# Post-norm decoder layer on one core: FFN sums placed ahead of the convolution wait, Winograd terms made by batch, and first loads of the output stage issued in the last attention group

## Chip, cores, metric

One Trainium2 chip, one core. The metric is the device time of one execution in microseconds, the median of the runs shown. All data are fp32 in DRAM; products on TensorE run in fp32 or, where a value is split in a high and a low part, as three products of parts (type fp32r).

## What is computed

The reference, cut to what matters. x is (4, 1024, 512), ctx (4, 2048, 512).

```python
def attn(x):                       # 32 heads of 16 columns, over 1024 tokens
    q = lin(lin(x, wq), vq); k = lin(lin(x, wk), vk); v = lin(lin(x, wv), vv)
    o = softmax(q k^T / 4) v       # laid out again so that heads become rows
    return lin(o, wo_w, wo_b)
def xattn(z1ss, uss, z0, weight, bias):
    z1h, z1c = z1ss[:, :512], z1ss[:, 512:]
    conv = causal conv of z1h along the last axis, 2 taps, 512 -> 2048 channels
    it, ot, gt, ft = split(uss + conv + bias, 4)
    ct = sigmoid(ft) * shifted(z1c) + sigmoid(it) * tanh(gt)
    return concat([sigmoid(ot) * tanh(ct), ct], axis=1)
def ffn(x):
    x_int = clip(round(x / scale), -127, 127)
    return (x_int * scale) @ (ternary_weight - 1).T + bias
x = layernorm(x + attn(x))
x = layernorm(x + xattn(x, ctx, z0, weight, bias))
x = layernorm(x + ffn(x))
```

## The kernel before, in words

`combine` and `project` make q, k and v. `attend` then runs 64 slots (a head of a pair of batches each) in 16 groups of four, the first and the last group written out and the middle ones in a loop. In each slot TensorE makes scores, DVE the negative maxima (L510), ACT the exponentials (L490), TensorE the products with v (L425), and ACT copies the result out (L479). Every pair of slots is also normalised beside this: `store_out` (L620) writes a result to DRAM, `load_pair` (L630, L634) reads its sums and its values back, DVE takes reciprocals (`recips`, L667), `load_recips` (L642, L645) sends them through DRAM to spread them over the partitions, and POOL multiplies and splits (`normalise`, L673 to L679). `store_parts` (L660) writes the parts. The last pair, number 31, is left to `finish`: its `load_pair` and `load_recips` are issued there by SP, its `recips` is DVE's first and its `normalise` one of POOL's first instructions.

The order in SP's queue is written out by hand. At the end of `attend`, behind the four slots of the last group, SP waits for v_ready and issues wo_raw (L386), then four loads of attention parts of 1 MB each (`load_o`, L687), the last `store_parts` of the even pairs and the last `store_out`. In `finish` it issues x tiles 0 to 3 (L830), wo_bias and z0s (L892, L893), x tiles 4 to 7, `load_pair`, three constants (L899), `load_recips`, the ternary weight (L901, into the buffer of the gates), attention parts for tiles 8 to 11, x tiles 8 to 15, the last `store_parts`, parts for tiles 12 to 15, two convolution weights (L843) and then the ctx tiles (L839).

`finish` has two passes p of two batches. A pass is a stage of 16 output tiles (`wo_stage`) and 16 convolution steps (`convs`).

In `wo_stage` TensorE makes a tile of 128 tokens x 512 columns with 12 products (L149) into one of six banks. POOL adds the bias to x (`add_wob`, L961), two tiles ahead of the tile that it normalises. DVE adds this to the bank (L1224), takes statistics (L1205, L1206); POOL makes the inverse deviation in four small instructions (`inv_std`, L952 to L957); ACT applies it (L1041). A ring of four y buffers ties them: DVE may start tile n once tile n - 4 is applied. In pass 1 the last FFN tiles of pass 0 stand between the output tiles, at places given by the tables `FFN_AFTER` (DVE, ACT, POOL) and `FFN_SLOT` (TensorE); x tiles of pass 1 are read into places that an FFN tile sets free, and their bias is added at the places of `X_AT`.

The convolution is done in Winograd form over pairs of columns. For each of four channel blocks c it needs x1's even and odd columns and two differences. POOL makes one difference (`last_term`, L989), DVE the other (`first_term`, L1256), ACT the high parts (`high_parts`, L1076, L1079), DVE the low parts (`low_parts`, L1262, L1266). One block covers both batches (128x512) and starts with tile 14; blocks 2 and 3 come behind tile 15. TensorE's first convolution waits for the blocks one by one (wx_made).

In `convs` step s makes gate g = s % 4 of channel block m = s // 4 (36 products, L149). DVE adds both Winograd halves to the ctx tile (L1302, L1305), ACT applies sigmoid or tanh (L1098); at g = 2 the cell is made (L1309 to L1311) and at g = 3 the hidden value (L1316), each followed by two normalisations (L1323 and on). FFN tiles q run along with an offset: DVE rounds x (`rounded`, L1215, L1216) at s - 3, ACT makes integers (L1048), TensorE turns them (L1127) at step s - 5, ACT copies them (`copy_turned`, L1054), TensorE multiplies with the ternary weight (L1137) at s - 6 of a later step, DVE adds (`out_of_ffn`, L1234), POOL adds the FFN bias to x (`add_ffb`, L967). TensorE waits before an FFN product for the copy and for DVE's sum of the tile before (there is one bank).

DVE, ACT and POOL each issue in program order, so an instruction that waits holds back all behind it.

## Time and profile before

| | us |
|---|---|
| median of 3 runs | 2242.64 |
| the runs | 2240.01, 2242.64, 2259.2 |
| the profiled execution | 2237.79 |
| its span, first to last instruction | 2236.1 |
| TensorE matmul busy | 2105.0 (94%) |
| VectorE busy | 1657.5 (74%) |
| ScalarE busy | 1312.2 (59%) |
| GpSimd busy | 483.6 (22%) |
| mean granted TensorE clock | 0.966 |

Times inside the kernel are counted from the span's start. Attention ends at 1735; the two output stages begin at 1736 and 1969. PE is TensorE's matmul, PEld its weight loads, DVE VectorE, ACT ScalarE, POOL GpSimd, SP the engine that issues the DMAs. A busy share of TensorE counts instructions in flight, also at a lowered clock.

### The profile page before, as it was taken

What the parts mean: (1) busy time and instruction counts of PE and PEld (TensorE: products, weight loads), DVE (VectorE), ACT (ScalarE), POOL (GpSimd) and SP (SyncE); (2) the same over time, 40 slices, a digit from 0 to 9 for tenths busy, and PEclk for the clock granted to TensorE, in tenths of its full rate; (3) what the DMA queues carried; (4) which work ended last, traced back from release to release, by engine and by line L of the source; (5) the groups of instructions that cost most, each with busy time, mean ns of one, the idle gap of its engine ahead of it and who ended that gap; (6) DMA issues with size and microseconds to landing.
All of it is one profiled execution on the core that took longest, in us unless ns stands there. A gap on an engine that the chain in (4) does not pass through costs nothing.

```text
span 2236.1 us, 39953 instructions
## 1 busy us (share of the span) xinstructions
PE 2105.0 (94%) x11304; PEld 1188.6 (53%) x11304; DVE 1657.5 (74%) x1693; ACT 1312.2 (59%) x2405; POOL 483.6 (22%) x964
## 2 busy tenths in 40 slices
PE   8999996999999999999999999999999888988895
PEld 3788883444444444444444444444443666766663
DVE  3333326888899899999999999999994466675676
ACT  0121110777888888888888888888888133343343
POOL 0000000112212212212212222222221523463243
PEclk9999995999999999999999999999999999999997
DMA  4355547364665665664665665565553957653662
GB/s 155 95 169 150 150 150 96 59 131 112 117 132 114 117 133 114 116 134 112 117 135 112 116 135 112 116 136 112 115 126 109 336 190 258 239 194 120 214 221 71
DMA packets 205962, 315.20 MB, mean 141 GB/s; under 512 B 105168, under 2 KB 105168, under 8 KB 193616
## 3 DMA queue, kind: packets, MB, share of 16 engines
q1 hardware_dynamic: 205904, 314.47, 55.0%
q8 instruction: 31, 0.51, 0.1%
q14 instruction: 27, 0.22, 0.0%
HBM read 211.06 MB, written 101.19 MB: 140 GB/s over the span
## 4 chain that ended last, share of the span: by engine, by line
PE 65%; DVE 7%; POOL 5%; SPq 2%; DMA 2%; issue 2%; ACT 2%; DVEq 0%; POOLq 0%; ACTq 0%
PE psum L416 25%; PE psum L425 22%; PE psum L398 10%; PE psum L149 7%; POOL rstd L955 1%; DVE neg_max L510 1%; POOL x L961 1%; DVE stats L1205 1%; ACT gates L1098 1%; SPq L317 1%; POOL var_eps L952 1%; POOL neg_mean_rstd L957 1%; DMA attended_dram<-out 1%; PE psum L1137 1%; SPq L323 1%
## 5 line engine op out<-in xcount | busy, mean ns | idle before, releaser
L510 DVE TENSOR_REDUCE neg_max<-psum 128x1 f32<-128x1024 f32 x1024 | 1205.0, 1219 | 141.5 <-PE psum L398 141.3
L490 ACT ACTIVATE probs<-psum 128x512 f32<-128x512 f32 x2048 | 1066.0, 605 | 312.7 <-PE psum L416 312.5
L416 PE MATMUL psum<-q_op,k_op 50*128 50x512 f32 x2048 | 757.6, 450 | 8.0 <-ACT probs L490 5.2
L416 PEld LDWEIGHTS psum<-q_op,k_op 50*128 50x128 f32 x2048 | 355.2, 192 | 585.9 <-ACT probs L490 575.6
L398 PE MATMUL psum<-k_op,q_op 48*128 48x512 f32 x2048 | 630.6, 488 | 21.8 <-DMA k_op<-qk_parts_dram 14.3
L425 PE MATMUL psum<-probs,v_op 128*32 128x512 f32 x4096 | 547.2, 606 | 1.6
L398 PEld LDWEIGHTS psum<-k_op,q_op 48*128 48x128 f32 x2048 | 388.7, 315 | 51.0 <-DVE neg_max L510 19.1
L149 PE MATMUL psum<-x_wino,conv_w 128*128 128x512 f32 x1152 | 278.4, 401 | 17.9 <-DVE x_wino L1266 17.3
L149 PEld LDWEIGHTS psum<-x_wino,conv_w 128*128 128x128 f32 x1152 | 220.9, 194 | 66.9 <-issue 16.9
L557 POOL CAST neg_max_parts<-neg_max 128x8 fp32r<-128x8 f32 x128 | 24.2, 189 | 807.2 <-DVE neg_max L510 807.2
L425 PEld LDWEIGHTS psum<-probs,v_op 128*32 128x32 f32 x4096 | 82.5, 108 | 130.5 <-issue 67.6
L230 ACT ACTIVATE qk_parts<-psum,qk_bias 128x512 fp32r<-128x512 f32 x64 | 44.0, 688 | 166.1 <-PE psum L149 166.0
L243 DVE SCALAR_TENSOR_TENSOR qk_parts<-psum,qk_bias,qk_parts 128x512 fp32r<-128x512 f32 x64 | 48.0, 750 | 120.1 <-ACT qk_parts L230 120.1
L1041 ACT ACTIVATE x<-y,neg_mean_rstd,rstd 128x512 f32<-128x512 f32 x64 | 52.2, 816 | 141.8 <-POOL neg_mean_rstd L957 141.8
L547 POOL COPY v_op<-values 128x256 f32 (+1 forms) x64 | 25.4, 397 | 456.0 <-issue 344.1
L149 PE MATMUL psum<-x_hi,w_hi 128*128 128x512 f32 x256 | 102.0, 398 | 5.0 <-ACTq L224 5.0
L1302 DVE TENSOR_TENSOR gates<-psum,gates 128x1024 f32<-128x1024 f32 x32 | 38.9, 1216 | 89.0 <-PE psum L149 89.0
L149 PE MATMUL psum<-x_lo,w_hi 128*128 128x512 f32 x256 | 101.7, 397 | 0.0
L149 PE MATMUL psum<-x_hi,w_lo 128*128 128x512 f32 x256 | 101.6, 397 | 0.0
L952 POOL TENSOR_TENSOR var_eps<-mean_var,eps 128x1 f32<-128x1 f32 x96 | 26.5, 276 | 248.0 <-DVE mean_var L1206 247.9
L673 POOL TENSOR_TENSOR o_raw<-o_raw,recips 128x512 f32<-128x512 f32 x32 | 41.0, 1280 | 166.0 <-DMA recips<-recips_dram 166.0
L1137 PE MATMUL psum<-tern,x_int_t 128*128 128x512 bf16 x128 | 39.3, 436 | 36.9 <-DVE y L1234 29.4
(96 smaller groups left out, 1656.6 us busy)
## 6 DMA issues: line engine op xcount, KB each, us to landing
q_op<-qk_parts_dram SPq DMA_DIRECT2D x384, 128.0 KB, 4.0
conv_w<-conv_w_parts_dram SPq DMA_DIRECT2D x32, 1536.0 KB, 7.1
qk_parts_dram<-qk_parts SPq DMA_DIRECT2D x128, 256.0 KB, 3.1
k_op<-qk_parts_dram SPq DMA_DIRECT2D x384, 64.0 KB, 3.9
conv_w_parts_dram<-conv_w_parts SPq DMA_DIRECT2D x16, 1536.0 KB, 6.1
attended_dram<-out SPq DMA_DIRECT2D x64, 256.0 KB, 2.1
attended_parts_dram<-o_parts SPq DMA_DIRECT2D x128, 128.0 KB, 2.2
gates<-in_ctx_dram SPq DMA_DIRECT2D x32, 512.0 KB, 3.6
```

The lines of the kernel that those rows point to most:

```text
L149: mm = nc.tensor.matmul(out, left, right, start=(first and i == 0), stop=(last and i == n - 1))
L230: nc.scalar.activation(parts[j % 4][:, 0, :], bank[j % 6], ACT.Identity, bias=qk_bias[:, j // KC, j % KC:j % KC + 1]).then_inc(qk_hi, 1)
L243: nc.vector.scalar_tensor_tensor(out=parts[j % 4][:, 1, :], in0=bank[j % 6], scalar=qk_bias[:, j // KC, j % KC:j % KC + 1], in1=parts[j % ...
L398: return nc.tensor.matmul(s1_bank[t % 2][:, lane * HALF:(lane + 1) * HALF], qop[i][r, b, t:S:QT], kop[i][r, b, :], start=True, stop=True)
L416: nc.tensor.matmul(s2_bank[cell % RING], kop[i][r, j // 2, n // 2 * P:(n // 2 + 1) * P], qop[i][r, j // 2, j % 2 * HALF:(j % 2 + 1) * HALF ...
L425: mm = nc.tensor.matmul(pv_bank[32 * j:32 * j + 32, :], vop[k % 2][:, j // 2 * QT + kt, :], probs[n % DEEP][:, j, :], start=(n == 0), stop ...
L490: nc.scalar.activation(probs[n % DEEP][:, j, :], s2_bank[cell % RING], ACT.Exp, scale=SCALE).then_inc(exp_done, 1)
L510: nc.vector.tensor_reduce(mx[b][:, t:t + 1], s1_bank[t % 2][:], AX_X, ALU.max, negate=True).then_inc(maxed, 1)
L673: nc.gpsimd.tensor_tensor(norm["o"][:], norm["o"][:], norm["den"][:], ALU.mult).then_inc(norm["o_made"], 1)
L952: G.tensor_tensor(veps[:, r:r + 1], mv[:, r, 1:2], eps[:], ALU.add).then_inc(prep, 1)
L1041: A.activation(dst, y[r][:], ACT.Identity, bias=nmr[:, r:r + 1], scale=rstd[:, r:r + 1]).then_inc(normed, 1)
L1137: mm = nc.tensor.matmul(bank[7], xit[q % 2][:, kc, :], wt[:, kc, :], start=(kc == 0), stop=(kc == KC - 1))
```

## The change

Three things are done. (1) In slot 62 (`last and k == 2`) SP issues wo_raw and the four loads of attention parts, which stood behind slot 63, and then wo_bias and the four x tiles of the first four output tiles, into a buffer of their own (x_first, which lies where the gates' buffer has its second half); the ternary weight is loaded behind slot 63, once wo_lo is made, and turned to bf16 by DVE at the end of `attend`. POOL adds the bias to the first four x tiles before it waits for anything else, and then stays three tiles ahead. (2) The Winograd terms are made for one batch at a time, in pieces of 128x256: batch 0's from tile 9 on, between the output tiles. (3) The FFN instructions of a convolution step stand at its start instead of at its end, DVE's sum ahead of its rounding and POOL's inverse deviation ahead of its bias addition, with the offsets raised by one; ACT's copy of the turned integers keeps its place beside the other two and so comes one convolution step later. The tables of the second output stage follow.

The core of the diff:

```diff
@@ attend, SP, in slot()
+                    if last and k == 2:
+                        sp.wait_ge(v_ready, SLOTS)
+                        sp.dma_start(late["wo_raw"][:], wo_t.rearrange("(c p) n -> p c n", p=P)).then_inc(late["wo_in"], DMA)
+                        sp.wait_ge(norm["parts_stored"], PAIRS // 2 * PART_STORES + DMA)
+                        for n in range(2):
+                            load_o(sp, late, on_scr, 0, n)
+                        sp.dma_start(late["wo_bias"][:], wo_b.broadcast_to([P, F])).then_inc(late["wo_bias_in"], DMA)
+                        for t in range(KC):
+                            sp.dma_start(late["x_first"][:, t, :], x_nat[0, (KC + t) * P:(KC + t + 1) * P, :])\
+                                .then_inc(late["x_in"], DMA)
@@ attend, SP, behind the slots
-                sp.wait_ge(v_ready, SLOTS)
-                sp.dma_start(late["wo_raw"][:], wo_t.rearrange("(c p) n -> p c n", p=P)).then_inc(late["wo_in"], DMA)
-                sp.wait_ge(norm["parts_stored"], PAIRS // 2 * PART_STORES + DMA)
-                for n in range(2):
-                    load_o(sp, late, on_scr, 0, n)
+                sp.wait_ge(late["wo_made"], 1)
+                sp.dma_start(late["tern_raw"][:], tern_t.rearrange("(c p) n -> p c n", p=P)).then_inc(late["tern_in"], DMA)
@@ attend, DVE, behind wo_lo
+                dve.wait_ge(late["tern_in"], DMA)
+                nc.vector.tensor_scalar(late["tern"][:], late["tern_raw"][:], -1.0, None, ALU.add)\
+                    .then_inc(late["tern_made"], 1)
@@ finish, tables
-    FFN_AFTER = ({}, {1: 16, 3: 17, 5: 18, 7: 19, 8: 20})
-    FFN_SLOT = ({}, {0: 16, 2: 17, 5: 18, 7: 19, 9: 20, 10: 21})
+    FFN_AT = ({}, {0: 16, 3: 17, 4: 18, 6: 19, 8: 20, 11: 21})
+    FFN_SLOT = ({}, {0: 16, 3: 17, 5: 18, 7: 19, 9: 20, 11: 21})
@@ finish, SP
-                for pos in range(4):
-                    load_x(0, *wo_tile(pos))
-                sp.dma_start(wob[:], wo_b.broadcast_to([P, F])).then_inc(wob_in, DMA)
-                sp.dma_start(z0s[:], z0).then_inc(wob_in, DMA)
                 for pos in range(4, 8):
                     load_x(0, *wo_tile(pos))
+                sp.dma_start(z0s[:], z0).then_inc(z0_in, DMA)
                 load_pair(sp, norm, us_scr, PAIRS - 1)
...
-                sp.dma_start(wi, tern_t.rearrange("(c p) n -> p c n", p=P)).then_inc(tern_in, DMA)
@@ finish, POOL
                 def ffn_part(p, s):
+                    if s >= 6:
+                        inv_std("ffn", p, s - 6)
                     if 0 <= s - 4 < TILES:
                         add_ffb(p, s - 4)
-                    if s >= 5:
-                        inv_std("ffn", p, s - 5)
...
                     for i, pos in enumerate(ORDER[p]):
-                        if p == 0 and i + 2 < TILES:
-                            add_wob(0, *wo_tile(i + 2))
+                        if p == 0 and 4 <= i + 3 < TILES:
+                            add_wob(0, *wo_tile(i + 3))
                         if p == 1 and i in X_AT:
                             add_wob(1, *ffn_tile(X_AT[i]))
+                        if i in FFN_AT[p]:
+                            ffn_part(p - 1, FFN_AT[p][i])
                         inv_std("wo", p, pos)
-                        if i in FFN_AFTER[p]:
-                            ffn_part(p - 1, FFN_AFTER[p][i])
-                        if i >= 14:
-                            last_term(p, i - 14)
-                    last_term(p, 2)
-                    last_term(p, 3)
+                        if i >= 9:
+                            last_term(p, (i - 9) // KC, (i - 9) % KC)
+                    last_term(p, 1, 3)
@@ finish, ACT
-                def ffn_first(p, s):
+                def ffn_part(p, s):
+                    if 0 <= s - 5 < TILES:
+                        copy_turned(p, s - 5)
                     if 0 <= s - 4 < TILES:
-                        copy_turned(p, s - 4)
-
-                def ffn_rest(p, s):
-                    if 0 <= s - 3 < TILES:
-                        integers(p, s - 3)
-                    if s >= 5:
-                        q = s - 5
+                        integers(p, s - 4)
+                    if s >= 6:
+                        q = s - 6
...
                 def convs(p):
                     for s in range(CONVS):
                         m, g = s // 4, s % 4
-                        ffn_first(p, s)
+                        ffn_part(p, s)
                         act.wait_ge(gate_in, p * CONVS + s + 1)
...
-                        ffn_rest(p, s)
@@ finish, TensorE, first convolution of a pass
-                                pe.wait_ge(wx_made, p * KC + c + 1)
+                                pe.wait_ge(wx_made, (2 * p + 1) * KC + c + 1)
@@ finish, DVE
                 def ffn_part(p, s):
-                    if 0 <= s - 3 < TILES:
-                        rounded(p, s - 3)
-                    if s >= 5:
-                        out_of_ffn(p, s - 5)
+                    if s >= 6:
+                        out_of_ffn(p, s - 6)
+                    if 0 <= s - 4 < TILES:
+                        rounded(p, s - 4)
...
                 def wo_stage(p):
                     for i, pos in enumerate(ORDER[p]):
+                        if i in FFN_AT[p]:
+                            ffn_part(p - 1, FFN_AT[p][i])
                         out_of_wo(p, pos)
                         if p == 0 and i == 5:
                             constants()
-                        if i in FFN_AFTER[p]:
-                            ffn_part(p - 1, FFN_AFTER[p][i])
-                        if i >= 14:
-                            first_term(p, i - 14)
-                    low_parts(p, 0)
-                    first_term(p, 2)
-                    low_parts(p, 1)
-                    first_term(p, 3)
-                    low_parts(p, 2)
-                    low_parts(p, 3)
+                        if i >= 10:
+                            low_parts(p, (i - 10) // KC, (i - 10) % KC)
+                        if i >= 9:
+                            first_term(p, (i - 9) // KC, (i - 9) % KC)
+                    low_parts(p, 1, 2)
+                    first_term(p, 1, 3)
+                    low_parts(p, 1, 3)
...
                 def convs(p):
                     for s in range(CONVS):
                         m, g = s // 4, s % 4
+                        ffn_part(p, s)
...
-                        ffn_part(p, s)
```

`first_term`, `low_parts`, `last_term` and `high_parts` take the batch bi as an argument and work on `x1[:, bi, c, ...]`, `tmp(bi, c, v)` and `wx[v][part][:, c, bi, :]`, each 128x256; wx_made counts 16 in place of 8. ACT's `high_parts` stand from tile 9 on too, behind the tile's own normalisation.

## Rows read from the trace of the kernel before

**Rows 1.** Busy time of each engine by stretch; columns: us, busy (instructions), PEclk, DMA share, GB/s.

```profile
1735.00:1790.00 55.00, 46.41 (x191) 37.86 (x192) 24.11 (x50) 10.18 (x13) 34.38 (x75) 0.91 0.89 327
...
1790.00:1811.00 21.00, 10.76 (x40) 8.07 (x39) 15.61 (x22) 9.86 (x16) 11.52 (x19) 0.84 0.12 38
```

**Rows 2.** The chain that ended last, 1735 to 1757; start us, us, what.

```profile
1735.40 8.12 DMA attended_dram<-out
...
1743.59 6.41 DMA sums<-attended_dram
...
1750.46 2.18 DMA recips_dram<-sums
...
1752.72 3.73 DMA recips<-recips_dram
...
1756.53 1.30 POOL o_raw L673
```

**Rows 3.** A quiet DMA queue before 1734: landing, two lines of the timeline, one stretch.

```profile
attended_dram<-out SPq DMA_DIRECT2D x1, 256.0 KB, 2.0
...
1700.03 0.67 SPq L630 DMA_DIRECT2D sums<-attended_dram  x1
...
1702.75 0.34 DVE L667 RECIPROCAL sums<-sums 128x32 f32<-128x32 f32 x1
...
1710.00:1714.00 4.00, 3.10 (x20) 1.06 (x16) 0.00 (x0) 2.93 (x7) 0.00 (x0) 1.00 0.00 0
```

**Rows 4.** POOL's timeline; then groups of 1735 to 1812 and one tile's (min/median/max ns).

```profile
1759.92 1.09 POOL L961 TENSOR_TENSOR x<-x,wo_bias 128x512 f32<-128x512 f32 x1
...
1788.58 1.09 POOL L961 TENSOR_TENSOR x<-x,wo_bias 128x512 f32<-128x512 f32 x1
...
L961 POOL TENSOR_TENSOR x<-x,wo_bias 128x512 f32<-128x512 f32 x16 | 18.9, 1187 | 10.6 <-DMA z0s<-in_z_dram 10.6
...
L1205 DVE BATCH_NORM_STATS2 stats<-y 128x6 f32<-128x512 f32 x16 | 11.1, 694 | 0.5
...
L1266 DVE TENSOR_TENSOR x_wino<-gates,x_wino 128x512 fp32r<-128x512 f32 x8 | 6.0, 784 | 0.0
...
L1291 DVE TENSOR_TENSOR scale<-scale 128x1 f32<-128x1 f32 x1 | 0.2, 158 | 0.0
...
L1266 DVE TENSOR_TENSOR x_wino<-gates,x_wino x8: 676/678/1525, 1797.4 to 1807.6; 128x512 fp32r<-128x512 f32 x8
```

**Rows 5.** DVE: the last tile of the first stage; all of L1302, first and last start.

```profile
1792.55 0.68 DVE L1224 TENSOR_TENSOR y<-psum,x 128x512 f32<-128x512 f32 x1
...
L1302 DVE TENSOR_TENSOR gates<-psum,gates x32: 1204/1223/1226, 1811.0 to 2203.8; 128x1024 f32<-128x1024 f32 x32
```

**Rows 6.** POOL and DVE at 2034.5, timeline.

```profile
2034.53 2.49 POOL L989 TENSOR_TENSOR gates<-x 128x512 f32<-128x512 f32 x2
...
2034.59 1.53 DVE L1256 TENSOR_TENSOR gates<-x 128x512 f32<-128x512 f32 x1
```

**Rows 7.** One group of four convolution steps, timeline.

```profile
1869.36 1.23 DVE L1302 TENSOR_TENSOR gates<-psum,gates 128x1024 f32<-128x1024 f32 x1 [4.42 <-PE psum L149]
...
1870.46 0.58 ACT L1054 COPY x_int_t<-psum 128x512 bf16<-128x512 bf16 x1 [3.37 <-PE psum L1127]
...
1881.53 1.86 PE L1137 MATMUL psum<-tern,x_int_t 128*128 128x512 bf16 x4 [2.84 <-DVE y L1234]
...
1881.70 0.81 ACT L1041 ACTIVATE x<-y,neg_mean_rstd,rstd 128x512 f32<-128x512 f32 x1 [0.54 <-POOL neg_mean_rstd L957]
...
1883.58 8.85 PE L149 MATMUL psum<-x_wino,conv_w 128*128 128x512 f32 x36
```

**Rows 8.** Second output stage, timelines of TensorE and DVE.

```profile
1977.82 1.02 PE L1137 MATMUL psum<-tern,x_int_t 128*128 128x512 bf16 x4 [2.74 <-DVE y L1234]
...
2015.60 0.69 DVE L1224 TENSOR_TENSOR y<-psum,x 128x512 f32<-128x512 f32 x1 [2.68 <-POOL x L961]
...
2046.72 1.22 DVE L1302 TENSOR_TENSOR gates<-psum,gates 128x1024 f32<-128x1024 f32 x1 [2.67 <-PE psum L149]
```

131 lines of the change are left out of this document (69 added, 62 removed).

## The prediction

> **What bounds the kernel now.** I read the busy time by stage first [rows 1]. Attention ends at 1735; behind it TensorE is still the fullest engine, so time can come only from stretches in which it sits idle or runs at the lower clock. The largest are the first output stage (46.4 of 55 us busy, granted clock 0.91) and the hand-over to the convolutions at 1790 to 1811 (10.8 of 21 us), which comes again in the second half. Within the convolutions TensorE loses a few us in each group of four steps.
>
> The chain of waits says why the first output stage is late [rows 2]: the last head's result takes 8.12 us to reach DRAM, its sums 6.41 us to come back, the reciprocals 2.18 and 3.73 us. POOL can scale that last head pair only at 1756.53, and every normalisation of the output stage is queued behind this multiplication on POOL. On a quiet queue the same transfers are short: the same store landed in 2.0 us, and sums issued at 1700.03 were there for the reciprocal at 1702.75; from 1710 to 1714 the DMA engines moved nothing [rows 3]. That is the hole the change fills. From 1760 POOL sets the pace: from the bias addition at 1759.92 to that at 1788.58 lie twelve tiles, so 2.4 us a tile, of which the addition is 1.19 and the inverse deviation 1.2 [rows 4].
>
> **Part 1, loads moved into the last attention group.** Moved to SP behind the last stored maxima (about 1706): the output weight, four loads of attention parts, the bias, four x tiles: 1 + 4 + 0.25 + 1 MB. The busy stretch moved 327 GB/s at a share of 0.89 [rows 1], so 0.37 MB a us at full share: 17 us, until about 1723. Then follow conv_w (1.5 MB), the ternary weight (1 MB) and the parts: drained near 1732. SP passes ten issues of about 1 us each, in a stretch in which it only waited for the result at 1717; the reciprocals of pair 30 come a few us later, with more than 5 us of slack. The added wait (wo_made) has the ternary load, one store_parts and the last store_out behind it; DVE, idle there, has made the weight parts by about 1713, so I take 0, with 1 us as the upper bound and 0 below, since nothing is taken off attention itself.
>
> What it buys: the last store finds a quiet queue and lands near 1737.5, before SP asks for it. SP issues four x loads and z0 first, until about 1739. Sums then take 2.7 to 3.5 us, so the reciprocal is at about 1742.2; 2.2 + 3.7 us for the recips put POOL's multiplication at 1748.3, 8.2 us sooner. Two additions that no longer stand behind it give 2 x 1.19 = 2.4. TensorE's stall before tile 8 goes too, but POOL is the bound there. POOL scales tile 8 at 1748.3 + 3.4 (the pair, 1756.53 to 1759.92) + 1.2 + 8 x 2.35 = 1771.7, and with ACT's 0.8 it is ready at 1772.5.
>
> **Part 2, Winograd terms by batch, inside the stage.** 16 DVE pieces of 128x512 a pass become 32 of 128x256, ACT 12 become 24, POOL 4 become 8. No such piece is in the trace. DVE's operation on 128x1 takes 0.16 us and an undisturbed whole piece 0.68, so half the elements make 0.16 + 0.26 = 0.42; bounds 0.34 (half of 0.68) and 0.78 (the mean of L1266 as it stands) [rows 4]. Four of them with one tile's sum and statistics (two of 0.69 and a short one, 1.6) make 3.3 us a tile on DVE from tile 10 on, more than POOL's or TensorE's pace. First pass: tile 10 is summed at 1773.5 (the first term waits for tile 8), tile 15 at 1773.5 + 5 x 3.3 = 1790. Before it was 1792.55, and the first gate sum, which shows the end of the first convolution, came 18.4 us later, at 1811.0 [rows 5]. Now only three groups are left behind tile 15: 1.6 for the tile, 3 x 1.7, the ACT and POOL steps between (1.7) and the last nine products (2.1) make 10.5. That gives 1800.5, a gain of 10.2 (the tail cut by 8, the tile 2.5 earlier).
>
> This assumes that DVE and POOL do not disturb each other. The trace shows that they do: POOL's term at 2034.53 and DVE's at 2034.59 run together, and DVE's took 1.53 us where 0.68 is usual [rows 6]. In the new stage POOL is nearly always busy beside these pieces. If all of them take turns, a tile costs 1.6 + 1.7 + POOL's 1.8 = 5.1 while additions still run and 4.2 behind, the first convolution ends near 1806.5 and the gain is 4.2. I take the middle, 7.2.
>
> The Trainium skill, SBUF — State Buffer, section Who interferes with whom, says that a DVE instruction with both inputs in SBUF contends with a GpSimd instruction that reads SBUF, and that one of the two blocks entirely. The pair just named agrees. By that rule alone the gain of this pass is 4.2, without it 10.2.
>
> **Part 3, second output stage.** Before, TensorE waits 2.74 us before its second FFN product, at 1977.82, and DVE waits 2.68 us for POOL's x addition at 2015.60, which stood behind the last FFN sum [rows 8]. These FFN sums now stand later in the order (TensorE's slots 3 and 11 in place of 2 and 10), so the first wait shrinks to under 1 us and the second is off that tile's way. Following the order with the measured durations, tile 7 is summed at 2007 and no longer at 2015.6. From there six tiles at 3.3 us bring tile 15 to 2026.7, and 10.5 us on, 2037.2 against 2046.7: 9.5 gained; with full turns 3.4. I take 6.5.
>
> **Part 4, FFN sums ahead of the convolution wait.** On DVE and POOL nearly nothing moves: what stood at the end of step s stands at the start of s + 1, only the two halves change places, and both were ahead of the wait already. On ACT one instruction does move: the copy of the turned integers is now behind the previous step's two normalisations. With the third gate's sum at 1869.36 this copy ran at 1870.46 [rows 7]. Now it runs when ACT is through with the cell's second normalisation, started at 1881.70, and so at 1882.4 to 1883.0. TensorE's FFN product, which started at 1881.53, starts at about 1883.0, 1.5 us later. The next convolution (1883.58 before) starts 0.8 to 1.5 later, or more if the longer idle time costs more of the low clock. Some of it is given back: the fourth gate's activation no longer has this copy before it (0.5), and 0.8 us of slack stand before the second step. Per group of four I take +1.1, bounds 0.2 and 2.2; there are four such groups (two in each half; the last of a half is in part 3 and the tail), so +4.4. The tail behind the last convolution: the copy costs it 1.0, POOL's inverse ahead of the addition gives as much back: 0.
>
> **The sum**: -7.2 - 6.5 + 4.4 = -9.3 on a profiled execution of 2237.8 us (span 2236.1), so 2228.5. The two lower timed runs are 2240.0 and 2242.6, mean 2241.3, so 2232; I say 2231.
>
> **Rivals.**
> *Clean interleave.* Pieces at 0.42 hardly meet POOL: -10.2 - 9.5 and +0.2 for each group make -19: 2222. For it: many POOL operations there are of 0.2 us; against it: rows 6.
> *Dear small pieces (slower).* A 128x256 piece costs what L1266 does in the mean today, 0.78 with its collisions. 64 pieces lie in DVE's chain; from my middle (about 0.51 each) that is 64 x 0.27 = +17, net +8: 2249. It decides from 9.3 / 64 = 0.15 above the middle, 0.66 us a piece. DVE's 0.16 for 128x1 speaks against it.
> *The copy costs more.* The longer idle time holds the clock low each time: 2.2 a group and 2 more at the start of the second output stage, so 4.4 + 2 more: net -3, 2238.
> *The loads do not bring the last pair sooner.* The x loads ahead of the sums fill the queue as before, POOL starts near 1756, and the first pass gains nothing: net -2, 2239.
>
> **How the numbers follow.** Forecast 0.47, clean 0.25, copy 0.13, dear pieces 0.08, loads 0.07. The range 2217 to 2244 holds the forecast's own bounds (-4.2 - 3.4 + 8.8 = +1.2 to -19) with some 3 us for the timing and all but the dear pieces. 1% is 22 us, about what can be told from no change; only the best of the clean case passes it, 0.1; slower by as much needs pieces dearer than any row, 0.03.
>
> **What would show it.** Right: POOL's last pair near 1748; no long stall before TensorE's tile 8; the first gate sum near 1804; in the fourth step the FFN product waits for ACT's copy, not for DVE's sum, and the third gate's sums of neighbouring groups lie 1 us further apart; 128x256 pieces near 0.42, some stretched to over 0.8. Wrong: gate sums no further apart than before (part 4), the first gate sum before 1801 (clean), or POOL's pair at 1756 (loads).

## The result, and the profile after

The changed kernel takes 2233.72 us (median of 12 runs, 2228.59 to 2239.26); the kernel before took 2247.77 us in the same comparison (12 runs, 2236.78 to 2259.2). The ratio on record is 0.9949, 95% interval 0.9931 to 0.9967 (it is not the quotient of the two medians, which is 0.9937). The profiled execution has a span of 2231.8 us, 4.3 below the 2236.1 of before. The forecast was 2231.0 in a range of 2217 to 2244, within 1%: it holds. Behind the total, though, several steps do not hold as they were told. All ratios of this document are of executions in the usual state; the only timed ones left out are two of e5, of 3016.65 and 9799.81 us.

The span alone hides where the time went. I read a ledger from one line instead, DVE's first gate sum of every convolution step (before L1302, now L1304): the first of a half shows the end of its output stage, the sixteenth the end of its convolutions. Attention differs by some us from one execution to the next, so the first stage is counted from the last maxima that POOL casts (before L557, now L567), which come ahead of all that was moved. The marks of that stretch, from the timelines of the two kernels. Before:

```profile
1703.03 0.19 POOL L557 CAST neg_max_parts<-neg_max 128x8 fp32r<-128x8 f32 x1 [7.98 <-DVE neg_max L510]
```

The gate sum of before stands in [rows 5], at 1811.0. After:

```profile
1705.18 0.19 POOL L567 CAST neg_max_parts<-neg_max 128x8 fp32r<-128x8 f32 x1 [7.98 <-DVE neg_max L517]
...
1808.22 1.23 DVE L1304 TENSOR_TENSOR gates<-psum,gates 128x1024 f32<-128x1024 f32 x1 [3.44 <-PE psum L149]
```

So the stretch fell from 108.0 to 103.0. The whole ledger, in us (forecast: the change of each term):

| stretch | before | after | change | forecast |
|---|---|---|---|---|
| last maxima to first gate sum | 108.0 | 103.0 | -5.0 | -7.2 |
| convolutions, first half | 156.6 | 159.7 | +3.1 | +2.2 |
| second output stage | 79.1 | 72.8 | -6.3 | -6.5 |
| convolutions, second half | 157.0 | 158.7 | +1.7 | +2.2 |
| behind the last gate sum | 32.3 | 32.4 | 0 | 0 |
| sum | | | -6.5 | -9.3 |

The spans differ by only 4.3 because attention up to those last maxima took 2.15 us more in this execution (1703.03, 1705.18).

**The first stage.** The two stretches that answer to [rows 1], with the same columns:

```profile
1735.00:1790.00 55.00, 49.70 (x209) 38.50 (x208) 26.84 (x56) 13.96 (x24) 40.76 (x81) 0.91 0.78 284
1790.00:1811.00 21.00, 13.88 (x50) 11.24 (x51) 15.28 (x34) 8.19 (x20) 9.04 (x22) 0.76 0.25 73
```

TensorE is busy for 3 us more in each stretch. What the moved loads cost stands in SP's queue and on POOL and DVE (the timeline of the changed kernel, 1720 to 1756):

```profile
1721.06 0.56 SPq L652 DMA_DIRECT2D recips_dram<-sums  x1
1730.34 0.69 SPq L655 DMA_DIRECT2D recips<-recips_dram  x1
1731.14 0.39 SPq L382 DMA_DIRECT2D conv_w_parts_dram<-conv_w_parts  x1
1731.58 0.42 SPq L396 DMA_DIRECT2D tern_raw<-in_tern_t_dram  x1
1738.34 1.78 SPq L670 DMA_DIRECT2D attended_parts_dram<-o_parts  x4
1740.17 0.43 SPq L630 DMA_DIRECT2D attended_dram<-out  x1
1742.40 1.78 SPq L839 DMA_DIRECT2D x<-in_x_dram  x4
...
1734.83 1.27 POOL L683 TENSOR_TENSOR o_raw<-o_raw,recips 128x512 f32<-128x512 f32 x1 [25.81 <-DMA recips<-recips_dram]
1755.83 1.29 POOL L683 TENSOR_TENSOR o_raw<-o_raw,recips 128x512 f32<-128x512 f32 x1 [6.38 <-DMA recips<-recips_dram]
...
1740.90 1.23 DVE L550 TENSOR_SCALAR tern<-tern_raw 128x2048 bf16<-128x2048 int32 x1 [23.42 <-DMA tern_raw<-in_tern_t_dram]
1748.43 0.35 DVE L677 RECIPROCAL sums<-sums 128x32 f32<-128x32 f32 x1 [6.30 <-DMA sums<-attended_dram]
```

A 16 KB store of reciprocals of pair 30 (L652) sits behind 6.25 MB of moved loads, and SP can issue their reload only 9.3 us later (1721.06, 1730.34; in four other profiles with these loads ahead of it 9.2 to 9.3); in [rows 2] a like store took 2.18 us. POOL scales pair 30 at 1734.83, SP stores its parts at 1738.34 and the last result at 1740.17, DVE turns the ternary weight at 1740.90, and the finish starts at 1742.40. From the last maxima that is 37.2 us; before it was 33.1 (SP's first x load at 1736.15). From the finish's start to POOL's multiplication of the last pair it is 13.4 us now and was 20.4. The forecast had 0 for the first (bound 1) and -8.2 for the whole; the whole was -2.9 (53.5 to 50.6, counted from the last maxima). From POOL's multiplication to the first gate sum it is 52.4 us now and was 54.5.

**The group of four.** The rows that answer to [rows 7], here from the second half (third gate's sum at 2098.6):

```profile
2111.21 0.56 ACT L1062 COPY x_int_t<-psum 128x512 bf16<-128x512 bf16 x1
...
2111.83 1.89 PE L1140 MATMUL psum<-tern,x_int_t 128*128 128x512 bf16 x4 [3.87 <-ACT x_int_t L1062]
2113.51 0.63 PE L1130 MATMUL psum<-ident,x_int 128*128 128x128 bf16 x4
```

The FFN product waits for ACT's copy and no longer for DVE's sum, as forecast, and the third gates' sums lie 43.8 to 44.1 us apart in the later groups (before 42.5 to 42.9).

### The profile page after: what moved, and what is told of

Its sections match the earlier page's. It is cut to its first block and busy times, and to the rows that moved or that the text cites. A ratio compares the mean times of both kernels' runs of the same rounds, so it can differ in the third digit from the quotient of the medians.

```text
span 2231.8 us, 40038 instructions
## 1 busy us (share of the span) xinstructions
PE 2111.3 (95%) x11304; PEld 1193.6 (53%) x11304; DVE 1659.0 (74%) x1725; ACT 1315.2 (59%) x2429; POOL 486.5 (22%) x972
## 3 DMA queue, kind: packets, MB, share of 16 engines
q1 hardware_dynamic: 205904, 314.47, 54.5%
## 5 line engine op out<-in xcount | busy, mean ns | idle before, releaser
L567 POOL CAST neg_max_parts<-neg_max 128x8 fp32r<-128x8 f32 x128 | 24.2, 189 | 808.9 <-DVE neg_max L517 808.9
L557 POOL COPY v_op<-values 128x256 f32 (+1 forms) x64 | 25.4, 397 | 457.8 <-issue 344.3
L1304 DVE TENSOR_TENSOR gates<-psum,gates 128x1024 f32<-128x1024 f32 x32 | 39.0, 1219 | 95.7 <-PE psum L149 95.7
L1103 ACT ACTIVATE gates<-gates,conv_bias 128x1024 f32<-128x1024 f32 x32 | 36.8, 1151 | 121.7 <-DVE gates L1307 121.6
```

Source lines behind the costliest of these rows:

```text
L1103: A.activation(gin[:, g, :, :], gin[:, g, :, :], ACT.Tanh if g == 1 else ACT.Sigmoid, bias=cb[:, col:col + 1]).then_inc(gate_out, 1)
L1304: steps.done(V.tensor_tensor(both, bank[4 + s % 2].rearrange("p (b i a) -> p b i a", b=2, a=1).broadcast_to([P, 2, HF, 2]), both, ALU.add))
```

## The experiments

All kernels are the changed one with one edit, unless said otherwise. One profile was read of each, so I give the ledger of all of them at once and show rows only where a verdict hangs on one. "Clock" is the granted clock at 1720 to 1736, the last slot of attention. "Third gates" are the distances between the third gate's sums of neighbouring groups, second and third distance of each half. What is left, behind the last gate sum, takes 32.0 to 32.8 us in all but e2 (30.7), e9 (31.5) and e5 (35.8).

| kernel | clock | maxima to gate sum | conv. 1 | second output stage | conv. 2 | third gates |
|---|---|---|---|---|---|---|
| before | 1.00 | 108.0 | 156.6 | 79.1 | 157.0 | 42.9 42.5, 42.7 42.8 |
| e7 before again | 0.55 | 114.4 | 156.7 | 77.9 | 157.2 | 42.9 42.5, 42.7 42.8 |
| after | 0.95 | 103.0 | 159.7 | 72.8 | 158.7 | 43.9 44.1, 43.8 44.1 |
| e1 after again | 0.56 | 108.6 | 158.9 | 72.9 | 158.8 | 43.2 44.3, 43.8 44.1 |
| e2 copy back | 0.56 | 108.4 | 158.9 | 73.1 | 158.0 | 43.2 44.2, 43.3 43.8 |
| e3 ternary late | 0.50 | 110.7 | 161.0 | 72.9 | 158.7 | 44.0 44.1, 43.9 44.1 |
| e4 whole pieces | 1.00 | 101.9 | 159.4 | 72.7 | 158.9 | 43.2 44.2, 43.9 44.1 |
| e5 order back | 0.57 | 108.5 | 160.5 | 75.1 | 160.4 | 45.3 44.4, 45.3 44.4 |
| e6 tables back | 0.50 | 113.5 | 160.7 | 76.0 | 159.0 | 44.2 44.3, 43.9 44.1 |
| e9 rounding, copy back | 0.50 | 114.8 | 157.2 | 75.0 | 156.7 | 43.3 43.0, 43.3 42.6 |
| e10 step order of before | 1.00 | 102.3 | 157.7 | 77.6 | 156.7 | 42.9 44.0, 43.2 42.5 |
| e12 loads behind | 0.50 | 110.1 | 158.4 | 72.8 | 156.5 | 43.2 44.1, 42.6 43.0 |
| e8 early FFN | 0.88 | 102.1 | 142.8 | 72.6 | 144.6 | 39.1 39.2, 39.3 39.0 |
| e11 early, ternary late | 1.00 | 102.1 | 143.4 | 72.6 | 146.3 | 39.2 38.8, 39.1 38.9 |

### Both kernels again

> The changed kernel once more, beside the kernel before, on one chip. It gives the scatter against which the next runs are read. My reading of the two profiles gives 4 to 5 us of gain in the profiled executions, the medians gave 11.5 us. If the profile of before was a low draw of its own scatter, this run lies at 0.993 to 0.997 of before again; if the profile was typical, at 0.998. The profile should show the first gate sum of each half near 1808 and 2041, and the third gate's sums 43.8 to 44.1 us after the third gate's sum of the group before in the two later groups of each half.

Measured: 2236.59 us, ratio 0.9961 (0.9939 to 0.9983), profiled span 2240.0. The ratio is within the range that was given, and the distances are near it (43.2 to 44.3), but the first gate sums of the halves came at 1816.9 and 2048.7 and not near 1808 and 2041. So I took the kernel before once more.

> The kernel before once more, for its profile. In the changed kernel's repetition TensorE ran the last slot of the attention at the lower of its two clock levels (granted 0.56 at 1720 to 1736, exponentials 4.07 us apart instead of 2.60) and the attention ended 11.5 us later than in the profile of the change, while in the profiles shown so far of before it did not. If that is a matter of the execution and not of the kernel, this profile can show it in the kernel before too, and its output stage, which waits for DRAM and POOL, then starts later by the same amount: span near 2248. If it belongs to the moved loads, this profile shows 1.00 at 1720 to 1736 again and a span within 3 us of 2236.

Measured: one run of 2248.33, span 2246.5. The windows of this profile (columns as in [rows 1]):

```profile
1700.00:1720.00 20.00, 17.71 (x106) 6.32 (x103) 7.33 (x7) 16.63 (x33) 3.54 (x6) 1.00 0.21 56
1720.00:1736.00 16.00, 14.77 (x52) 3.66 (x48) 0.76 (x1) 9.06 (x18) 3.14 (x3) 0.55 0.68 241
1736.00:1750.00 14.00, 12.82 (x48) 3.35 (x44) 2.77 (x2) 6.55 (x13) 0.00 (x0) 0.53 0.77 287
```

and ACT's exponentials in it (timeline):

```profile
1724.67 2.08 ACT L490 ACTIVATE probs<-psum 128x512 f32<-128x512 f32 x4 [1.31 <-PE psum L416]
1728.74 2.08 ACT L490 ACTIVATE probs<-psum 128x512 f32<-128x512 f32 x4 [1.99 <-PE psum L416]
```

Four exponentials (one row each) come 4.07 us after the last four; in the first profile of before it was 2.60. TensorE, 99.9% busy from 1600 to 1700 and 89% from 1700 to 1720, drops to its lower level (granted 0.55, so near 1.2 GHz of 2.4) and becomes the bound of the last slot. It happens with both orders of loads: 8 of the 14 profiles show 0.50 to 0.57 there, one of the two of before among them, the others 0.88 to 1.00. The first gate sum is then 6.4 us later in the kernel before (108.0, 114.4) and 5.6 in the changed one (103.0, 108.6). Compared like with like, the change brings 5.0 and 5.8 us in this stretch, and the spans, less the time to the last maxima, differ by 6.5 and 6.8. The medians say 11.5 (7 to 16 by the interval) and in the second comparison 8.8 (4 to 14); what of that is more than 6.6 no profile here explains. The timed runs beside the experiments say more than two medians: the kernel before ran 87 times there, mean 2245.2 us, the changed one 24 times in all, mean 2236.0, both at a mean granted clock of 0.960. That is 9.2 us. Nearly all of the scatter of before goes with the clock of the execution: a straight line through its 87 runs has 14.5 us for each 0.01 (correlation -0.95), and the changed kernel's two sets lie 9.2 and 10.1 us below this line (my estimate, from the times and clocks of the runs).

The first output stage of the like profiles, cut at the finish's start (SP's first x load of the finish) and at POOL's multiplication of the last pair, with two experiments that follow:

| kernel | clock | maxima to finish's start | to POOL's last pair | to first gate sum |
|---|---|---|---|---|
| before | 1.00 | 33.1 | 20.4 | 54.5 |
| after | 0.95 | 37.2 | 13.4 | 52.4 |
| e4 whole pieces | 1.00 | 37.3 | 13.5 | 51.1 |
| e7 before again | 0.55 | 43.0 | 16.9 | 54.5 |
| e1 after again | 0.56 | 43.0 | 13.6 | 52.0 |
| e12 loads behind | 0.50 | 44.8 | 12.8 | 52.5 |

Where the last slot runs at the lower level, attention ends so late that the burst no longer holds back the finish (43.0 in both kernels), and in the kernel before the last pair then follows 16.9 us behind the finish's start instead of 20.4.

### Whole pieces in place of half ones

```diff
-                        if i >= 9:
-                            last_term(p, (i - 9) // KC, (i - 9) % KC)
-                    last_term(p, 1, 3)
+                        if i >= 14:
+                            last_term(p, i - 14)
+                    last_term(p, 2)
+                    last_term(p, 3)
```

(and so for ACT's and DVE's terms).

> Only the Winograd terms by batch are undone: whole pieces of 128x512 from tile 14 on, as before; the moved loads and the FFN order stay. My reading (the interleaved pieces slow the last tiles by as much as the shorter tail gives back in the first pass; in the second the FFN order alone would leave the tail at 18.4 us): first gate sum of the first half within 2 us of 1808.2, tile 15 of it summed 6 to 8 us sooner and the convolution's end 18 us behind it instead of 11.0; second output stage longer by 3 to 5 us. Rival A (the pieces carry the whole gain of both stages, and loads and order little): both first gate sums 7 us or more later, 14 us in all. Rival B (the pieces bring nothing, all gain of the second stage is the FFN order): the second stage within 1 us too, and the time that of the changed kernel.

Measured: ratio 0.9968 (0.9945 to 0.9991), span 2230.1. The first stage is as my reading had it; for the second it is rival B, where I had 3 to 5 us more. Both output stages are as long as with half pieces (101.9 and 72.7 against 103.0 and 72.8). DVE's rows, whole pieces:

```profile
1789.44 0.68 DVE L1231 TENSOR_TENSOR y<-psum,x 128x512 f32<-128x512 f32 x1
...
1794.23 1.48 DVE L1263 TENSOR_TENSOR gates<-x 128x512 f32<-128x512 f32 x1
1795.63 1.52 DVE L1268 TENSOR_TENSOR x_wino<-x,x_wino 128x512 fp32r<-128x512 f32 x1
...
1801.76 0.68 DVE L1268 TENSOR_TENSOR x_wino<-x,x_wino 128x512 fp32r<-128x512 f32 x1
...
1806.30 1.22 DVE L1307 TENSOR_TENSOR gates<-psum,gates 128x1024 f32<-128x1024 f32 x1 [2.66 <-PE psum L149]
```

and half pieces in the changed kernel (the last DVE row and POOL's stand side by side in time):

```profile
1780.02 0.63 DVE L1259 TENSOR_TENSOR gates<-x 128x256 f32<-128x256 f32 x1 [4.96 <-ACT x L1049]
1780.57 0.68 DVE L1228 TENSOR_TENSOR y<-psum,x 128x512 f32<-128x512 f32 x1
...
1784.23 0.41 DVE L1259 TENSOR_TENSOR gates<-x 128x256 f32<-128x256 f32 x1
1784.56 0.68 DVE L1228 TENSOR_TENSOR y<-psum,x 128x512 f32<-128x512 f32 x1
...
1797.22 0.68 DVE L1228 TENSOR_TENSOR y<-psum,x 128x512 f32<-128x512 f32 x1
...
1788.75 1.27 POOL L967 TENSOR_TENSOR x<-x,wo_bias 128x512 f32<-128x512 f32 x1
...
1789.42 0.88 DVE L1265 TENSOR_TENSOR x_wino<-x,x_wino 128x256 fp32r<-128x256 f32 x1
```

Tile 15 is summed at 1789.44 with whole pieces and 1797.22 with half ones, and the gate sum follows 16.9 and 11.0 us later. With half pieces the last tiles follow each other on DVE at some 3.3 us instead of 2.4, and the first piece waits 4.96 us for a tile that ACT has not yet normalised. Of the 64 half pieces 56 take 0.39 to 0.43 us; beside them POOL runs only operations on 128x1, or none. The other eight take 0.62 to 0.88, and they are just the eight that overlap one of POOL's operations on 128x512 or 128x256, as the last two rows show. A whole piece takes 0.68, or 1.48 and 1.52 beside POOL's terms. Part 2 moves time inside the stage and saves none.

### The loads

```diff
-                    if last and k == 2:
-                        sp.wait_ge(v_ready, SLOTS)
-                        sp.dma_start(late["wo_raw"][:], wo_t.rearrange("(c p) n -> p c n", p=P)).then_inc(late["wo_in"], DMA)
...
                 for k in range(4):
                     slot(LAST, k, last=True)
 
+                sp.wait_ge(v_ready, SLOTS)
+                sp.dma_start(late["wo_raw"][:], wo_t.rearrange("(c p) n -> p c n", p=P)).then_inc(late["wo_in"], DMA)
...
```

(with the parts, the bias and the four x tiles behind it, and the ternary weight in the finish as in the next edit).

> All moved loads go back behind the last slot (wo_raw, the four parts, bias, four x tiles), and the ternary weight into the finish; the POOL order, the pieces and the FFN order stay as changed. Theory (the loads make the whole gain of the first output stage, the pieces nothing): from TensorE's first output product to the first gate sum 71 to 75 us, as in the two profiles of before (71.2 and 74.7), instead of 64 to 66; time 5 to 8 us above the changed kernel. Rival (POOL's bias additions ahead of everything, three tiles in advance, make the gain): 66 to 68 us.

Measured: 2241.65 us, ratio 0.9995 (0.9963 to 1.0026). The median is 5 to 8 us above the changed kernel's, as expected. In the profile, though, the first output product stands 65.1 us ahead of the gate sum, where I had 71 to 75: the theory falls in this execution. But TensorE ran at 0.50 in its last slot (and at 0.82 before that), so that attention left the loads some 10 us more. Against the other profiles with such a slow last group (110.7, 113.5, 114.8) its 110.1 is no loss, and against the 114.4 of before it is a gain. In the two stretches behind the finish's start it equals the changed kernel (12.8 and 52.5; 13.6 and 52.0 in e1). So there the gain needs none of the loads in slot 62. What e12 keeps of part 1 is that bias and four x tiles no longer stand in the finish's queue ahead of the last pair's sums (from ACT's last copy to DVE's reciprocal 11.8 us in e7, 7.15 here, 7.3 in e1), and POOL's bias additions ahead and three tiles in advance; no run takes these two apart. Whether slot 62 is worth something when the last slot runs at the full clock was not seen in a profile. The ratio hints that it is, but it overstates it: these eight runs had a mean clock of 0.957, and by the line through the runs of before they are 6.9 us faster than it at their clocks, against 9.2 and 10.1 for the changed kernel. That leaves some 3 us for the moved loads (an estimate).

The other half is the ternary weight.

```diff
-                sp.wait_ge(late["wo_made"], 1)
-                sp.dma_start(late["tern_raw"][:], tern_t.rearrange("(c p) n -> p c n", p=P)).then_inc(late["tern_in"], DMA)
...
                 load_recips(sp, norm, r_scr, PAIRS - 1)
+                sp.dma_start(late["tern_raw"][:], tern_t.rearrange("(c p) n -> p c n", p=P)).then_inc(late["tern_in"], DMA)
```

(DVE's conversion goes into the scale constants.)

> Only the ternary weight goes back: SP loads it in the finish, behind the reciprocals of the last pair, and DVE turns it to bf16 in the scale constants; all other moved loads stay. My theory (DVE's conversion at the end of attention waits until about 1740.9 for a load that lies behind all the moved loads, and holds back the finish): the finish starts about 4 us sooner (TensorE's first output product at 1738 to 1739 instead of 1742.6), POOL's multiplication of the last pair at 1751 to 1752 instead of 1755.8, the first gate sum 3 to 4 us sooner. Rival A (the same queue holds back something else that comes as late, the last stored result or the x tiles): product and multiplication come under 1 us sooner and the time stays. Rival B (the ternary load, now between the reciprocals and the attention parts, makes tiles 8 to 11 late as before): the start is 4 us sooner, but TensorE waits at tile 8 and the first gate sum comes less than 1.5 us sooner.

Measured: ratio 0.9943 (0.9921 to 0.9965), no difference from the changed kernel's. The profile could not answer: the last slot ran at 0.50, and ACT's last copy came at 1748.56, later than DVE turns the weight in any profile that loads it early (1737.6 to 1744.1). The same edit on top of the early FFN parts (below) caught a profile at 1.00. There the finish starts 35.6 us after the last maxima instead of 37.2, held by the other chain alone:

```profile
1722.99 0.56 SPq L647 DMA_DIRECT2D recips_dram<-sums  x1
1732.27 0.69 SPq L650 DMA_DIRECT2D recips<-recips_dram  x1
...
1740.20 1.75 SPq L665 DMA_DIRECT2D attended_parts_dram<-o_parts  x4
1741.99 0.44 SPq L625 DMA_DIRECT2D attended_dram<-out  x1
1742.83 0.87 SPq L839 DMA_DIRECT2D x<-in_x_dram  x2
```

and the gate sum comes at 102.1, against 103.0, 101.9, 102.3 and 102.1 of the four profiles with the early load and a last slot at 0.88 or more. So of the 4.1 us by which the finish starts late, 1.6 are the ternary weight and 2.5 the reciprocals of pair 30 behind the burst; and the 1.6 are worth nothing at the end of the stage.

### The order inside a convolution step

```diff
-                    if 0 <= s - 5 < TILES:
+                    if CONVS < s and s - 5 < TILES:
                         copy_turned(p, s - 5)
...
                         ffn_part(p, s)
+                        if s >= 4:
+                            copy_turned(p, s - 4)
                         act.wait_ge(gate_in, p * CONVS + s + 1)
```

> Only ACT's copy of the turned integers goes back to where it stood in the convolution steps: one step earlier, behind the integers and the FFN's apply and ahead of the wait for the gate sum. My theory (the copy behind the two normalisations of the third gate makes the FFN product and with it the next cold convolution late): the distances between neighbouring third-gate sums fall from 43.8-44.1 to at most 42.9, TensorE's product no longer names ACT's copy as what it waited for, and the run is 4 to 5 us shorter than the changed kernel; both output stages stay within 1 us. Rival A (the order of DVE's sum and rounding, or POOL's inverse ahead of its bias addition, costs the time): distances stay at 43.8 or more and the time stays. Rival B (TensorE waits for DVE's sum in place of the copy): the wait only changes its name, distances near 43.4, gain under 2 us.

Measured: ratio 0.9951 (0.9926 to 0.9977), within the noise of the changed kernel's 0.9949 and 0.9961; distances 43.3 and 43.8 in the second half, a half's convolutions 158.0 to 158.9. The theory (42.9 at most, 4 to 5 us) falls; it is rival B, and less than it gave:

```profile
2117.88 1.87 PE L1142 MATMUL psum<-tern,x_int_t 128*128 128x512 bf16 x4 [2.01 <-DVE y L1240]
2120.34 0.61 PE L1132 MATMUL psum<-ident,x_int 128*128 128x128 bf16 x4 [0.60 <-ACT x_int L1056]
```

The product starts 11.3 us after the third gate's sum instead of 13.2, but the turn waits for the integers, which come later because DVE now rounds behind its sum, and in this group all runs at the lower clock.

```diff
-                    if s >= 6:
+                    if s >= 6 and s > CONVS:
                         out_of_ffn(p, s - 6)
                     if 0 <= s - 4 < TILES:
                         rounded(p, s - 4)
+                    if 6 <= s <= CONVS:
+                        out_of_ffn(p, s - 6)
```

(on top of the copy; on POOL likewise the addition ahead of the inverse)

> Inside the convolution steps the whole FFN order goes back: the copy a step earlier as in the run before, DVE's rounding ahead of its sum, POOL's bias addition ahead of the inverse deviation. The output stages keep the changed order. With the copy alone back, the FFN product started at 11.4 us after the third gate's sum instead of 13.2, but the turn then waited for the integers until 13.84, and the convolution behind it ran at the lower clock. My theory now: the sum ahead of the rounding is the other half of the price, since it makes the integers of the fourth step late; with both back, the distances between the later third-gate sums return to 42.4 to 42.9 (before: 42.5 to 42.9; changed: 43.8 to 44.1; copy alone: 43.2 to 44.2), TensorE's wait in the group is again for DVE's sum (near 2.8 us), and a half's convolutions take 157 us instead of 159. Rival: the distance follows the granted clock alone, which falls in one kernel and not in another by where the idle time happens to lie; then the product stands at the place of before, 12.2 us, but runs 1.9 us long, and the distances stay at 43.5 or more.

Measured: ratio 1.0 (0.9976 to 1.0024), distances 45.3 and 44.4: slower than either. The edit was not the order of before: POOL's bias addition had kept the raised tile number, so that ahead of the inverse it waited for integers just being made. POOL, and ACT behind it:

```profile
2124.16 1.28 POOL L978 TENSOR_TENSOR x<-x,ffn_bias 128x512 f32<-128x512 f32 x1 [1.54 <-ACT x_int L1058]
...
2126.73 0.82 ACT L1051 ACTIVATE out<-y,neg_mean_rstd,rstd 128x512 f32<-128x512 f32 x1 [2.64 <-POOL neg_mean_rstd L963]
```

It shows what POOL's inverse-first order is for: e9 below differs from it in this order alone, and in e5 the two groups take 2.0 and 1.4 to 1.8 us more.

The next two have the copy and DVE's rounding back; e9 leaves POOL as changed, and e10 puts it back with the tile number:

```diff
                 def ffn_part(p, s):
+                    if 5 <= s <= CONVS:
+                        add_ffb(p, s - 5)
                     if s >= 6:
                         inv_std("ffn", p, s - 6)
-                    if 0 <= s - 4 < TILES:
+                    if CONVS <= s < TILES + 4:
                         add_ffb(p, s - 4)
```

> In the convolution steps the copy a step earlier and DVE's rounding ahead of its sum, as before the change; POOL keeps the changed order (inverse first, then the addition for the tile whose integers have just been made). The last run that put the order back also put POOL's addition ahead of the inverse while its tile number stayed the raised one, so POOL waited 1.5 us for ACT's integers, the gate's activation came at 17.6 us instead of 15.7, and the distances grew to 44.4 and 45.3. My theory (the copy and the sum ahead of the rounding are the price of the FFN order): distances 42.5 to 42.9 again, a half's convolutions 157 us. Rival (POOL's order counts as well, through the FFN inverse or through the later addition): distances 43.2 or more.

> As the run beside it, and POOL also as before the change in the convolution steps: bias addition first, and for the tile one behind (whose integers are a step old). That is the order of before in full, with the output stages as changed. Both theories expect distances of 42.5 to 42.9 and convolutions of 157 us a half; with the output stage at 72.8 the second half then is some 2 us shorter than in the changed kernel and the first 2 to 3. If the distances stay above 43, the price is not in the order inside the steps at all but in what the changed output stages hand over.

Measured: ratios 0.9946 (0.9914 to 0.9978) and 0.9979 (0.9948 to 1.0009). Both bring the convolutions back to 157 (157.2, 156.7; 157.7, 156.7), as expected. The distances are 42.5 to 43.3 and one of 44.0, so only in part those of the theory (42.5 to 42.9). But e9 gives its gain back in the second output stage (75.0) and e10 more (77.6). First convolutions and second output stage together: before 235.7 and 234.6; changed 232.5 and 231.8; e2 232.0; e9 232.2; e10 235.3. So the copy and DVE's order only move time from one stretch to the other, and the 3 us that stay hang on POOL's part: inverse first, addition a step earlier. They hang on the places of the FFN tiles as well: with the old places (e6, below) the same sum is 236.7. Neither carries them alone.

What the price in the convolutions is made of shows in windows over one stall (end of one convolution to the gate sum of the next but one, second group of the second half). After, then e12, which has the same order in these steps:

```profile
2107.90:2123.70 15.80, 11.93 (x46) 8.73 (x46) 12.53 (x23) 8.19 (x11) 9.26 (x26) 0.78 0.67 237
```

```profile
2110.40:2124.50 14.10, 9.31 (x44) 7.26 (x44) 12.40 (x22) 6.50 (x9) 7.84 (x24) 1.00 0.69 250
```

With a granted clock of 0.78 the third gates lie 43.8 us apart, with 1.00 they lie 42.6 apart. In the next group it is 0.78 and 44.1 against 0.88 and 43.0. The kernel before had 1.00 and 0.88 in these two and distances of 42.7 and 42.8. In the changed kernel and in e12 the product starts 13.2 us or more behind the third gate's sum. The other groups of this order fit: 43.2 near 0.89 (the first group shown of e1, e4 and e12), 43.8 to 44.3 near 0.78. So the late product by itself costs little; nearly all of the 1.1 us a group is the lower level of the clock in the convolution behind the longer idle time, and an execution can escape it. This rests on a comparison of executions: no run sets the clock. Why e12 escaped it is open.

### The places in the second output stage

```diff
-    FFN_AT = ({}, {0: 16, 3: 17, 4: 18, 6: 19, 8: 20, 11: 21})
-    FFN_SLOT = ({}, {0: 16, 3: 17, 5: 18, 7: 19, 9: 20, 11: 21})
+    FFN_AT = ({}, {0: 16, 2: 17, 4: 18, 6: 19, 8: 20, 9: 21})
+    FFN_SLOT = ({}, {0: 16, 2: 17, 5: 18, 7: 19, 9: 20, 10: 21})
```

> Only the places of the FFN tiles in the second output stage go back: DVE, ACT and POOL take them ahead of tiles 0, 2, 4, 6, 8, 9 (changed: 0, 3, 4, 6, 8, 11) and TensorE ahead of 0, 2, 5, 7, 9, 10 (changed: 0, 3, 5, 7, 9, 11). Whole pieces in place of half ones left this stage at 72.7 us, so the gain of 6.3 us in it does not come from the pieces. My theory (the places): TensorE's wait before its second FFN product (2.7 us before the change) and DVE's wait for POOL's last addition (2.7 us) come back, and the stage takes 76 to 79 us instead of 72.8. Rival (the order inside an FFN part, POOL's inverse ahead of its addition and DVE's sum ahead of its rounding, makes the gain at any place): the stage stays within 1 us of 72.8.

Measured: ratio 0.9978 (0.9962 to 0.9995); the stage takes 76.0, at the lower end of what was expected: the places carry 3.2 of the 6.3 us. But the two waits by which the theory told it do not come back: TensorE waits 1.54 us before its second FFN product (2.74 before the change) and DVE 0.18 for POOL's last addition (2.68). The rest goes with the order inside the FFN part (75.0 and 77.6 in e9 and e10, whose tables are the new ones). Pieces carry none (72.7 in e4).

### A version that beats both

```diff
+    def moved(s):
+        return 0 < s < CONVS and s % 4 in (3, 0)
...
-                        ffn_part(p, s)
+                        if not moved(s):
+                            ffn_part(p, s)
...
                                         ALU.add).then_inc(gate_in, 1)
+                        if moved(s + 1):
+                            ffn_part(p, s + 1)
                         if g == 2:
```

(DVE; the same on ACT behind the gate's activation and on POOL ahead of the step's inverses, and in the list that numbers the normalisations.)

> A version to beat both, on top of the changed kernel: in the steps of the third and fourth gate, DVE, ACT and POOL do the FFN part of the next step right behind the gate's sum (ACT behind the gate's activation), ahead of the cell or hidden value and its two normalisations, and no longer behind them. TensorE's order stays. Theory (TensorE's wait in the group, 3.9 us for ACT's copy, and the slow convolution behind it, 9.8 instead of 8.5 us, both come from the FFN part being queued behind the cell): the FFN product then starts as the convolution before it ends, the third gates' sums lie near 4 x 9.37 = 37.5 us apart instead of 43.8 to 44.1, 6.4 us in each of the seven later groups of the two halves, about 40 us in all with the first ones: near 2195. Rival A (DVE's later gate sum becomes the bound, since the FFN part delays the cell by 1.3 us): distances near 41, near 2212. Rival B (the clock falls anyway): distances near 43, under 8 us of gain.

Measured: 2210.08 us (six runs), ratio 0.9858 (0.9826 to 0.9891), span 2202.5. Beside the change's 0.9949 and 0.9961 that is another 1%, though not the 2195 of the theory.

```profile
2079.15 1.04 PE L1151 MATMUL psum<-tern,x_int_t 128*128 128x512 bf16 x4
2080.03 0.39 PE L1141 MATMUL psum<-ident,x_int 128*128 128x128 bf16 x4
2080.22 8.46 PE L149 MATMUL psum<-x_wino,conv_w 128*128 128x512 f32 x36
2088.52 1.04 PE L1151 MATMUL psum<-tern,x_int_t 128*128 128x512 bf16 x4
...
2086.59 2.19 DVE L1327 TENSOR_TENSOR gates<-gates 128x1024 f32<-128x1024 f32 x1
...
2091.90 1.21 DVE L1316 TENSOR_TENSOR gates<-psum,gates 128x1024 f32<-128x1024 f32 x1
```

The product follows the convolution at 9.2 us after the third gate's sum without a wait, at the full clock: the theory's mechanism. The distance in this group is 39.3 and not 37.5, and two waits of TensorE for the convolution weight make 1.5 of the difference:

```profile
2099.89 8.42 PE L149 MATMUL psum<-x_wino,conv_w 128*128 128x512 f32 x36 [0.75 <-DMA conv_w<-conv_w_parts_dram]
...
2110.14 2.08 PE L149 MATMUL psum<-x_wino,conv_w 128*128 128x512 f32 x8 [0.72 <-DMA conv_w<-conv_w_parts_dram]
```

DVE's gate sum at 2091.90 comes late, since the FFN part and an operation of 2.19 us (1.22 is usual) lie ahead of it, but TensorE does not wait for it. The median is rival A's number, 2212, without its mechanism; the profile, at 2202.5, is between the two.

> The early FFN parts (2210 us median, span 2202.5 in its profile) with the ternary weight loaded late as in the third run. Theory (DVE's wait for the ternary weight holds back the finish only where attention ends at the full clock, near 1736 to 1742, because the weight lands near 1741 whatever attention does): the median is 0 to 4 us below 2210, and where the profile has the last slot at the full clock, TensorE's first output product starts within 2 us of ACT's last copy, as it does where the last slot ran slowly, instead of 4 to 6. Rival (the load among the finish's own loads costs as much there): the time from that first product to the first gate sum grows from 65 to 68 us or more, and the median is that of the early FFN parts or above.

Measured: 2210.56, ratio 0.9858 (0.9819 to 0.9898): the same. The theory falls: the first output product starts 3.5 us behind the end of ACT's last copy and not within 2, for pair 30's reciprocals hold the finish (above). From that product to the gate sum it is 66.3 us, under the rival's 68.

## Why the prediction held, point by point

- **The total.** That it lies so near is in part luck. The forecast took its -9.3 from 2241.3, the mean of two of three runs; in the comparison the kernel before had a median of 2247.8, 6.5 higher, and from there the forecast would be 2238.5 against the measured 2233.7. The profiles of like clock have -6.5 and -6.8, the 87 and 24 timed runs -9.2. In the ledger two terms are right by steps other than those told (parts 2 and 3).
- **Part 1, attention's end at 0 (bound 1).** This step failed. It costs 4.1 us where the last slot runs at the full clock, and nothing where it does not (43.0 and 43.0). SP's ten issues took 12 us where I had priced about 10 (1708.19 to 1720.27), but I gave the reciprocals of pair 30 "a few us" with slack; they came 9.3 us later and with them the parts store and the last result. The ternary load behind the burst was not followed at all.
- **Part 1, the last pair 8.2 us sooner.** 2.9 us, for that reason. POOL's last pair started at 1755.83, which is what I had named as the sign that the loads fail (1756, against 1748 if they work); 2.15 us of that is the later attention of this execution. From the finish's start on it is 7.0 less, near the forecast. The sums wait and the recips took what the quiet rows gave (DVE's reciprocal 3.6 us after the issue of the sums).
- **Part 2.** Behind POOL's last pair the forecast was right for undisturbed pieces: 52.2 us to the first gate sum (1748.3 to 1800.5), measured 52.4. The size of a piece (0.42, measured 0.39 to 0.43), the pace of 3.3 us a tile and the tail of 10.5 (measured 11.0) hold. What I had wrong was how often POOL's long operations meet the pieces: eight of 64, so that the 3 us held back for it were not needed. So -7.2 became -5.0 by two errors: the pair 5.3 us less early than told, and the 3 us of turns that did not come. (By my own marks the two bounds are 10.5 and 4.5, not 10.2 and 4.2.) And I never asked what whole pieces would give with the same loads: the same, as e4 shows, for the half pieces slow the tiles ahead by as much as they shorten the tail. That the stage's gain is due to what part 1 moved follows from that by elimination; the run that undoes the loads (e12) does not show it in its profile, only in its times.
- **Part 3.** -6.5 forecast, -6.3 and -5.0 measured: that the number fits is luck. None of it is the pieces, which I had given six tiles and a tail. About half goes when the old places come back, without the two waits that I had followed, and in the changed kernel itself DVE still waits 2.67 us for POOL's addition at that tile (sum at 2009.41, forecast 2007). The other part is the order inside the FFN part, POOL's above all, which I had counted nowhere.
- **Part 4.** +4.4 forecast, +4.8 and +3.8 measured, with ACT's copy as the wait, as told. But the copy is not the price: put back, it gives at most 0.5 us a group. The price is the clock, 0.78 where the kernel before and e12 had 0.88 to 1.00, behind a longer idle time, which I had as a condition ("more if the longer idle time costs more of the low clock") and which is nearly all of it. In the tail the copy does cost something, as told: with it back (e2) the stretch behind the last gate sum is 30.7 and not 32.4.
- **Rivals.** Clean pieces were there, without the gain of that case; pieces dear throughout, and full turns, are excluded by the 56 of 64 at 0.43 or less. "The loads do not bring the last pair sooner" came true in its first half, nearly (2.9 us of 8.2), and not in its second: the first stage still gained 5.0.

## What to carry to other kernels

A small store or reload that others wait for must not stand behind megabytes in the same queue: look at every such small round (here 16 KB) that is late in a stage before filling the "quiet" stretch ahead of it. Finer interleaving of work that the same engine has to do anyway only moves its wait; ask what the first piece waits for. Where an engine's in-order queue has short independent work behind a long chain (here FFN parts behind the cell and its two normalisations), moving the short work ahead of the chain brought some 25 us; it also kept TensorE at its full clock (1.00 in the four later groups). The orders within the short work differed by 3.5 us in all from the first gate sum to the end (after, e2, e9, e10: 420.5 to 424.0), apart from e5, which cost 8 more by a wait of its own making.
